# An LSTM followed by a convolution and a scan: the last pieces of the second layer laid out anew, a polynomial logarithm, one scan per 128 columns

## What is computed

```
# layer 0: LSTM, 512 strictly serial steps
a = x_t @ Wx + b + h @ Wh            # Wh: 512 x 2048
i, f, o = sigmoid(a[:3 blocks]); g = tanh(a[last block])
c = f*c + i*g ; h = o*tanh(c)
y = x + h
# layer 1: 8-tap convolution per feature (taps are the 8 rows of cond), projections, a first-order scan
conv = conv_b + sum_k y[t-7+k] * cond[k]
B_t, C_t = softplus(conv @ Wp[:, :64] + bp), tanh(conv @ Wp[:, 64:] + bp)
u = y @ Ws + bs                       # 64 states
s = decay*s + dt*B_t*u ; z = C_t*s
out = y + z @ Wo + bo
```

## Time and profile before

| | |
|---|---|
| median of three runs | 1904.51 us |
| the profiled execution | 1906.64 us, its span 1904.8 us, 1.84 us outside the span |
| TensorE matmul busy | 1812.7 us, 95% |
| VectorE busy | 1426.2 us, 75% |
| ScalarE busy | 1120.7 us, 59% |
| GpSimd busy | 337.9 us, 18% |
| mean granted TensorE clock | 0.993 of full |

### The profile page before, as it was taken

How to read it: one execution, slowest core, us unless ns; L and a number is a source line. 1 busy time by engine, 2 the same in 40 slices (tenths; PEclk the granted TensorE clock), 3 DMA queues, 4 the chain that set the end, 5 groups by cost and what they waited for, 6 DMA issues and landing times.

```text
span 1904.8 us, 124385 instructions
## 1 busy us (share of the span) xinstructions
PE 1812.7 (95%) x52738; PEld 1421.0 (75%) x52738; DVE 1426.2 (75%) x7431; ACT 1120.7 (59%) x4565; POOL 337.9 (18%) x1544
## 2 busy tenths in 40 slices
PE   6888999999999999999999999999999999999976
PEld 3666777777777777777777777777777777777865
DVE  8787667777777777777777777777777787867675
ACT  5655565565656656565565656566555566656453
POOL 1111111111111111111111111111111111111110
PEclk9999999999999999999999999999999999999997
DMA  6111111111111211111111111111111121211100
GB/s 235 55 46 39 50 49 44 47 56 41 54 54 40 63 46 51 54 46 54 46 57 46 55 48 48 55 51 54 45 54 51 41 62 44 66 38 52 44 19 20
DMA packets 112292, 100.74 MB, mean 53 GB/s; under 512 B 20225, under 2 KB 86069, under 8 KB 110710
## 3 DMA queue, kind: packets, MB, share of 16 engines
q1 hardware_dynamic: 111448, 90.70, 15.7%
q10 hardware_dynamic: 288, 2.10, 0.3%
HBM read 50.77 MB, written 41.94 MB: 49 GB/s over the span
## 4 chain that ended last, share of the span: by engine, by line
PE 72%; DVE 11%; ACT 11%; issue 3%; POOL 2%; DMA 1%; SPq 0%; POOLq 0%; DVEq 0%; ACTq 0%
PE recA L546 27%; PE recB L553 16%; PE pw L505 12%; PE pbc L630 12%; ACT act L831 5%; DVE tr L954 4%; ACT recA L757 3%; DVE pre L963 2%; POOL h L472 2%; DVE hz L989 2%; ACT tc L846 1%; PE pu L603 1%; PE pw L489 1%; PE po L650 1%; DMA wpk<-in_L_cond_Wh_dram 1%
## 5 line engine op out<-in xcount | busy, mean ns | idle before, releaser
L831 ACT ACTIVATE act<-pre 128x64 f32<-128x64 f32 (+1 forms) x1024 | 255.7, 250 | 720.0 <-DVE pre L963 712.2
L553 PE MATMUL recB<-wlo,hz 128*32 128x128 f16 x16352 | 577.8, 219 | 1.4 <-issue 1.4
L553 PE MATMUL recB<-whi,hz 128*32 128x128 f16 x16352 | 577.6, 219 | 0.7 <-issue 0.7
L546 PE MATMUL recA<-whi,hz 128*16 128x256 f16 x8176 | 515.8, 274 | 59.6 <-DVE hz L989 51.0
L546 PE MATMUL recA<-wlo,hz 128*16 128x256 f16 x8176 | 512.6, 273 | 0.1
L553 PEld LDWEIGHTS recB<-whi,hz 128*32 128x32 f16 x16352 | 438.1, 97 | 9.5
L553 PEld LDWEIGHTS recB<-wlo,hz 128*32 128x32 f16 x16352 | 438.2, 97 | 4.1 <-issue 1.9
L546 PEld LDWEIGHTS recA<-whi,hz 128*16 128x16 f16 x8176 | 199.9, 88 | 288.2 <-DVE hz L989 265.8
L954 DVE STREAM_TRANSPOSE tr<-recA 128x256 f32<-128x256 f32 x512 | 229.8, 449 | 201.0 <-PE recA L546 198.8
L630 PE MATMUL pbc<-yt,wpk 128*128 128x256 f32 (+5 forms) x1120 | 330.8, 401 | 0.0
L472 POOL TENSOR_TENSOR h<-osc,tc 128x16 f32<-128x16 f32 x1024 | 226.8, 221 | 450.2 <-ACT tc L846 450.2
(11 more groups left out here) (166 smaller groups left out, 2167.2 us busy)
## 6 DMA issues: line engine op xcount, KB each, us to landing
xw_rows<-xs SPq DMA_DIRECT2D x128, 256.0 KB, 2.3
seed<-xw_rows SPq DMA_DIRECT2D x1008, 32.0 KB, 2.0
xn<-in_x_dram SPq DMA_DIRECT2D x32, 256.0 KB
out_dram<-ot SPq DMA_DIRECT2D x32, 256.0 KB, 3.0
seed<-in_L_cond_Wh_dram ACTq DMA_DIRECT2D x2, 1024.0 KB, 7.0
wpk<-in_L_cond_Wh_dram SPq DMA_DIRECT2D x2, 1024.0 KB, 12.7
wlo<-in_L_cond_Wx_dram SPq DMA_DIRECT2D x2, 1024.0 KB, 13.9
xs<-in_L_cond_Wx_dram SPq DMA_DIRECT2D x1, 1024.0 KB, 10.1
```

Source lines behind the costliest of these rows:

```text
L546: ins = pe.matmul(rec[0][32 * j:32 * j + 2 * NB, 0:256].rearrange("p (c f) -> p c f", c=2), h[:, 2 * NB:4 * NB], w[:, k, :, :].rearrange(" ...
L553: ins = pe.matmul(rec[1][32 * j:32 * j + 32, 0:128], h[:, 2 * NB * (1 - c):2 * NB * (1 - c) + 32], w[:, k, 4 * (2 + c) + j, :], start=Fals ...
L831: act_eng.activation(act[q][:, q:G, :].rearrange("p g n -> p (g n)"), pre[q][:, q:G, :, :].rearrange("p g c b -> p (g c b)"), ACT.Tanh, sc ...
```

## The change

What it does:

1. The logarithm becomes a polynomial of degree 10 in s itself: `top` and nine `term` with fitted constants, then `sum`. `den`, `rcp`, `w`, `w2` are gone.
2. `drive` writes its product batch by batch instead of step by step. A new instruction `carry` adds decay times the last state to the first column of each batch. The scan then runs from zero over 128 columns at once; its multiplier row `dec` is zero at each batch's first column. A 256-column piece has two scans, a half piece one. `ys` reads the states back with strides.
3. The last y additions are at t = 507 (four steps), 509 (two), 510 and 511 (one each).
4. The convolutions of pieces 13 and 14 are given as 64 matmuls of 128 columns instead of 32 of 256. The last piece has 32 matmuls of 128 columns, in order of their taps: 5, 6, 7 and 10 in slots 508 to 511, and 4 in slot 512, the last tap, ahead of `y_u`.
5. The last pieces get slots of their own (the table `NEAR_END`), ScalarE's and VectorE's jobs are placed one by one against their costs, and the projections of the last groups move with `pe_load`. Worked out from the planner's code, the lists differ from slot 396 on:

| | before | after |
|---|---|---|
| conv 12, slots | 421 to 436 (2 each) | 419 to 427 (2), 428 to 441 (1) |
| conv 13 | 453 to 468 (2) | 445 to 466 (3 halves each) |
| conv 14 | 482 to 492 (3) | 471 to 490 (3 halves), 491 (5 halves) |
| `y_u` of piece 14 | 483 (all four) | 488 to 491 |
| VectorE jobs of piece 14 | 494 to 500 | 494 to 502 |
| conv 15 | 496 to 502 (5) | 495 to 501 (5) |
| VectorE jobs of piece 15 | 503 to 507 | 502 to 510 |
| most projections in one slot, 469 to 491 | 8 | 6 |
| output of steps 496 to 511 | slots 509, 510 and 513, 517 | slots 508, 513 and 513, 514 |

6. In the last slot ScalarE takes `abs` and `sig` before `u`.

Its core:

```diff
+    LOG1M = (1.0, 0.5000016093254089, 0.3332335352897644, 0.25240495800971985, ...)
+    SERIES = len(LOG1M) - 1
...
+        def y_steps(t):
+            if t >= T - 2:
+                return [t]
+            if t == T - 3:
+                return [t - 1, t]
+            return list(range(t - HS + 1, t + 1)) if (t + 1) % HS == 0 else []
...
         def conv_order(i):
             n, a, e, cols = span(i)
-            if i < NP - 1:
-                return [(c, k, a, e) for k in range(TAPS) for c in range(KC)]
-            reach = [min(e, e - HS + TAPS - 1 - k) for k in range(TAPS)]
-            return ([(c, k, a, reach[k]) for k in range(TAPS) for c in range(KC)] +
-                    [(c, k, reach[k], e) for k in range(TAPS) for c in range(KC) if reach[k] < e])
+            taps = [(c, k) for k in range(TAPS) for c in range(KC)]
+            size = TB if i < LAST - 1 else TT
+            return [(c, k, lo, lo + size) for lo in range(a, e, size) for c, k in taps]
...
-            return ["abs", "sig", "pos"], ["den"] + ["rcp"] * rcp_parts(key) + ["w", "w2", "top"] + ["term"] * SERIES + ["sum"]
+            return ["abs", "sig", "pos"], ["top"] + ["term"] * SERIES + ["sum"]
...
-            return ["u"] + on_act + ["c"] + on_dve + ["drive"] + ["scan"] * NB + ["ys"]
+            on_act = ["u"] + on_act + ["c"] if i < NP - 1 else ["abs", "sig", "u", "pos", "c"]
+            return on_act + on_dve + ["drive", "carry"] + ["scan"] * (span(i)[3] // 128) + ["ys"]
...
+        NEAR_END = {LAST - 2: ([(0, 18, 3, 2), (18, 32, 12, 1)], 20, 26, 0.65),
+                    LAST - 1: ([(0, 64, -3, 3)], 12, 18, 0.65),
+                    LAST: ([(0, 32, -9, 3), (32, 59, 2, 3), (59, 64, 11, 5)], 8, 12, 0.9),
+                    LAST + 1: ([(0, 32, -1, 5)], 2, 5, 0.8)}
...
+                conv_when[i] = [(0, 5, T - 4, 5), (5, 11, T - 3, 6), (11, 18, T - 2, 7), (18, 28, T - 1, 10),
+                                (28, jobs, T, KC)]
...
                 if name == "drive":
...
-                    dve.scalar_tensor_tensor(sp[:, 0:cols], sp[:, 0:cols], dtv[:, 0:1], us[:, 0:cols],
-                                             ALU.mult, ALU.mult).then_inc(s_drive, 1)
+                    dve.scalar_tensor_tensor(by_batch(acc[:, 0:cols]), by_step(sp[:, 0:cols]), dtv[:, 0:1],
+                                             by_step(us[:, 0:cols]), ALU.mult, ALU.mult).then_inc(s_drive, 1)
+                elif name == "carry":
+                    if i:
...
+                        first = acc[:, 0:cols:e - a]
+                        dve.scalar_tensor_tensor(first, st[:, (i - 1) % 2, ahead - 1:NB * ahead:ahead], decay[:, 0:1], first,
+                                                 ALU.mult, ALU.add).then_inc(s_drive, 1)
                 elif name == "scan":
...
-                    ins = dve.tensor_tensor_scan(st[:, i % 2, 0:e - a, z], dec[:, 0:e - a], sp[:, z:cols:NB], init,
+                    some = slice(128 * z, 128 * z + 128)
+                    ins = dve.tensor_tensor_scan(st[:, i % 2, some], dec[0 if e - a == TB else 1][:, :], acc[:, some], 0.0,
                                                  ALU.mult, ALU.add)
```

More of the change, by code:

```diff
@@ L87, in lstm_ssm_kernel @@
         sg = sb("sg", [N, COLS])
-        w2 = sb("w2", [N, COLS])
         acc = sb("acc", [N, COLS])
         ct = sb("ct", [N, COLS])
-        st = sb("st", [N, 2, TB, NB])
+        st = sb("st", [N, 2, COLS])
         ys = sb("ys", [N + 1, 2, COLS])
-        dec = sb("dec", [N, TB])
+        dec = [sb(f"dec{z}", [N, 128]) for z in range(2)]
         dtv = sb("dtv", [N, 2])
@@ L237, in lstm_ssm_kernel @@
                 dve_load[ev_when(g) + 2 + part] += 0.34
-        DVE_COST = {"den": 0.33, "rcp": 0.46, "w": 0.34, "w2": 0.34, "top": 0.34, "term": 0.44, "sum": 0.44,
-                    "drive": 0.44, "scan": 0.2, "ys": 0.35}
+        DVE_COST = {"top": 0.34, "term": 0.44, "sum": 0.44,
+                    "drive": 0.44, "carry": 0.1, "scan": 0.4, "ys": 0.35}
+        DVE_COST_HALF = {"top": 0.25, "term": 0.32, "sum": 0.32, "drive": 0.38, "carry": 0.2, "scan": 0.46, "ys": 0.3}
         ACT_AT = {"u": 0, "abs": 1, "sig": 1, "pos": 2, "c": 2}
@@ new lines, in lstm_ssm_kernel @@
+            base = TB * n + e
+            if i == NP - 1:
+                conv_when[i] = [(0, 5, T - 4, 5), (5, 11, T - 3, 6), (11, 18, T - 2, 7), (18, 28, T - 1, 10),
+                                (28, jobs, T, KC)]
+                u_when[i] = [T] * KC
+                post_at[i] = [T + 1] * len(post_order(i))
+                slot = T + 2
+                continue
+            if i in NEAR_END:
+                conv_plan, u_first, slot, room = NEAR_END[i]
+                conv_when[i] = [(lo, hi, base + first, rate) for lo, hi, first, rate in conv_plan]
+                u_when[i] = [base + u_first + k for k in range(KC)]
+                slot += base
+            else:
+                conv_when[i] = [(0, 13, base + 3, 1), (13, 21, base + 16, 2), (21, jobs, base + 20, 1)]
+                u_when[i] = [base + 27 + k for k in range(KC)]
+                slot, room = base + 31, 0.65
@@ new lines, in lstm_ssm_kernel @@
+            act_at = ACT_AT if e - a == TB else {"u": 0, "abs": 0, "sig": 0, "pos": 1, "c": 1}
+            if i == LAST - 1:
+                act_at = dict(ACT_AT, c=4)
+            post_at[i] = [slot + act_at[name] for name in post_order(i)[:len(act_at)]]
+            slot += act_at["pos"]
+            for name in post_order(i)[len(act_at):]:
+                cost = (DVE_COST if e - a == TB else DVE_COST_HALF)[name]
+                while dve_load[slot] + cost > room:
+                    slot += 1
+                dve_load[slot] += cost
+                post_at[i].append(slot)
@@ L270, in lstm_ssm_kernel @@
+            if n < NBLK - 6:
+                slot = base + 60
+            elif i not in NEAR_END:
+                slot += 3
+            elif i == LAST - 1:
+                slot = base + 43
+            elif i == LAST:
+                slot -= 1
+            for z in range(2):
+                if TT * z < e and a < TT * z + TT and (a <= TT * z):
+                    slot = min(slot + 3, T - 1)
                     while evacuates(slot):
                         slot += 1
-                    out_when[n, z] = (slot - 2, slot - 1, slot)
@@ L273, in lstm_ssm_kernel @@
[L273 to L292, removed]
+                    out_when[n, z] = (slot - 2, slot - 1, slot) if e - a == TB else (T - 4, T + 1, T + 1)
@@ L628, in conv @@
                 if last >= 0:
-                    pe.wait_ge(s_yadd, (TB * n + last) // HS + 1)
+                    pe.wait_ge(s_yadd, y_done(TB * n + last))
                 ins = pe.matmul(pbc[:, NB * (lo - a):NB * (hi - a)], wpk[:, k, c, :],
@@ L656, in beside @@
                 for i in range(NP):
+                    for lo, hi, first, rate in conv_when[i]:
+                        for j in due(t, first, rate, hi - lo):
+                            conv(i, lo + j)
                     for k in range(KC):
@@ L992, in output @@
             def output(t):
-                n = t // TB
+                n, steps = t // TB, y_steps(t)
                 if t == HS - 1:
@@ L997, in output @@
                     dve.wait_ge(s_xlow, 2 * n + 1)
[L998 to L1001, removed]
+                at = HALO + NB * (steps[0] % TB)
+                y = yt[:, n % XR, :, at:at + len(steps) * NB]
+                first = steps[0] % HS
+                dve.scalar_tensor_tensor(y, h32[:, :, first:first + len(steps), :].rearrange("p k s b -> p k (s b)"),
+                                         0.5 / SC, y, ALU.mult, ALU.add).then_inc(s_yadd, 1)
             def y_halo(n):
@@ L1024, in soft @@
                 S = lambda a: a[:, 0:cols]
-                if name == "den":
+                if name == "top":
                     dve.wait_ge(s_ssig, key + 1)
[L1027 to L1040, removed]
+                    dve.tensor_scalar(S(acc), S(sg), LOG1M[SERIES], None, ALU.mult).then_inc(s_ser, 1)
                 elif name == "term":
@@ L1122, in _ @@
             dve.memset(ys[N:N + 1, :, :], 1.0).then_inc(s_ones, 1)
-            dve.memset(dec[:, :], 1.0).then_inc(s_dec, 1)
+            for z in range(2):
+                dve.memset(dec[z][:, :], 1.0).then_inc(s_dec, 1)
+            dve.wait_ge(s_dec, 2)
+            for z in range(2):
+                dve.memset(dec[z][:, 0:128:TB >> z], 0.0).then_inc(s_dec, 1)
             for q in range(2):
```

80 lines of the change are left out of this document (29 added, 51 removed).

## The result

The changed kernel takes **1896.18 us** (median of five runs, 1895.59 to 1897.25) against 1904.87 (five runs, 1903.36 to 1908.45). The ratio is 0.9953, with a 95% interval of 0.9938 to 0.9967. It is faster, by 0.47% instead of the 0.98% forecast, and lies outside the forecast's range. The profiled execution took 1895.59 us, its span 1893.7.

The account below looks back on a forecast made before the run. The prediction took the 3.53 us recurrence loop through TensorE, VectorE, ScalarE and GpSimd as the bound. Its terms summed to -19.0 us, 0.3 given back: -18.7, from median 1904.51 to 1885.8 us, range 1881.5 to 1892.0.

Parts of the forecast that it names:

- The sign: Whole kernel: faster by over 3.8 us at 96%, within that 1%, slower 3%.
- the place of the gain: Mid-kernel closed to this change, bound by the 3.53 us recurrence; the end is where it can act.
- the forecast's five terms: Slots 482 to 492 -2.2 us, 493 to 501 -3.9, 502 to 507 -4.3, 508 to 510 -1.9, tail -6.7.
- The TensorE formula: Every step: the larger of 3.53 us and 2.07 plus 0.235 per projection, 0.43 per convolution, 0.22 per half, and other jobs.
- The tail: From the last transposition to the end: 4.8 + 4.7 + 6.0, given as 15.6 us against 22.3, -6.7.
- The rival with exposed weight loads: Slots 445 to 465 and 471 to 490: a half convolution costs like a whole, 0.43 us; +26 us, 1912; 3%.
- The 428 ns for a half convolution: Half convolutions: 2 x (107 + 107) ns by the skill's weight-load rule; the prediction held the row with 0.22 us against it.
- Up to slot 395: Slots up to 395: TensorE lists the same, VectorE's changed list hidden by its idle time; no change in time.
- to get going: Projections behind the recurrence's block in a step: about 0.2 us once, then 0.235 each.
- The clock: Rival, slots 492 to 508: clock falls, two to five half-clock steps at 0.9 us each; 1887.5 to 1890.5; 10%.
- A new queue wait: Rival: piece 14's first convolution waits for piece 13's late `c`, or strided writes cost double; 1890 to 1894; 8%.
- the polynomial alone counts: Rival, tail: narrow convolutions were hidden already, so the tail gives only 2 us; 1890; 2%.

Follow-up runs that it names:

- e8: Changed kernel with `y_u` split in two portions, one behind the convolutions, one behind the slot's first projection (or at the slot's end): 1922.53 us, ratio 1.0097.
- e1: Changed kernel with `y_u` ahead of the convolutions again in all slots but the last (512): 1887.43 us, ratio 0.9908 to the kernel before.
- e4: Kernel before with only the last convolution's part (32 matmuls of 128 columns, its y additions, `y_u` behind it in slot 512): 1899.45 us, ratio 0.9983.
- e3b: Kernel before with only polynomial, `carry` and 128-column scans, output slots pinned to those before: 1902.39 us, ratio 1.0000.
- e3: Kernel before with only polynomial, `carry` and 128-column scans, output slots left to the planner: 1915.20 us, ratio 1.0056.
- e5: Changed kernel with `y_u` of slots below 512 last in its slot, behind the projections: 1886.10 us, ratio 0.9898 to the kernel before.
- e9: Kernel before with the new VectorE instructions and the last convolution with its y additions, on the old plan: 1898.26 us, ratio 0.9973.
- e2: Kernel before with only the convolutions of a slot moved ahead of its `y_u` (slot 512 keeps the old order): 1912.34 us, ratio 1.0035.

## Why the prediction was wrong

**The sign, the place of the gain and the end were right.** Slots 482 to 510 and the tail gained 138.5 - 121.2 = 17.3 us; the forecast's five terms there sum to 19.0. The TensorE formula (2.07 plus 0.235, 0.43 and 0.22 for each job) met the new slots: three halves with four projections were forecast at 3.67 and took 3.67 or 3.68. (The tail's sum 4.8 + 4.7 + 6.0 is 15.5, not 15.6.) The rival with exposed weight loads is out by that. The 428 ns for a half convolution were the prediction's estimate, which adds load and matmul. The Trainium skill, "TensorE: Matmul & The Clock Gate", section "LDWEIGHTS (loading the stationary operand)", gives the duration of a load alone; the trace does not agree with adding it, as a half convolution takes 0.22 us here.

**The failed step is the term "Up to slot 395": "The TensorE lists are the same. ... Nothing."** The lists were the same, their order within a slot was not. The jobs of a slot were compared as sets; the hunk in TensorE's `beside` that turns them was not priced. Nor would the prediction's formula have shown it, as it charges the 0.2 "to get going" once a slot. e8 shows that it is paid at each return from narrow to wide matmuls: 0.43 against 0.23. Undone, it gives the kernel 0.9953 - 0.9908 = 0.45% or 8.6 us, of the 10.4 by which the forecast of 1885.8 was missed. By the two intervals that difference is good to about 4 us; the steps of the two traces say 7.8, which is surer. e1's 1887.43 lies 1.6 above the forecast.

**The same "Nothing" was wrong on VectorE too, by less.** The prediction took the new list for hidden because it fits. The long steps at fixed places sum to 3.6 us with the new VectorE program and to 1.9 with the old, +1.7, though the list fits. That e1 still met 1190.2 against 1190.4 in slots 60 to 394 is luck of the profiled execution before with its long steps at 91, 118 and 379; e4, with the old VectorE program and the old order, took 1187.9.

**The tail** is right by its steps: 3.42 us for the 14 half convolutions of slots 511 and 512 together, ScalarE's `abs` at 1882.02 - 1877.80 = +4.2 (forecast +4.1), VectorE at +5.0 (+4.8), `top` to `ys` 5.0 (4.7: `drive`, `carry` and `ys` were each taken 0.06 to 0.08 too cheap, the rest by less), and 6.0 from there. The changed kernel's chain, with the lines left out that repeat nine times:

```profile
1878.52 3.42 PE pbc L645 x28
...
1882.02 0.37 ACT av L777
...
1882.76 0.23 DVE acc L1043
...
1886.18 0.43 DVE acc L1065
...
1887.35 0.38 DVE ys L1090
...
1887.77 1.97 PE po L665 x4
```

**The rivals.** The clock did not fall in slots 492 to 508 (granted clock 1.00); it stood at 1.00 up to the final `ys` and was 0.52 over the output matmuls and what follows them. Before, it had fallen earlier, from 1888 us on, under the narrow convolutions. So part of the 5.06 us that the change took away was half clock: the same records took 3.70 in e3b. After:

```profile
1882.00:1887.70 5.70, 2.23 (x24) 1.50 (x22) 4.46 (x15) 2.50 (x7) 0.00 (x0) 1.00 0.17 46
1887.70:1893.70 6.00, 1.96 (x4) 1.07 (x4) 0.02 (x1) 0.60 (x1) 0.00 (x0) 0.52 0.17 44
```

A new queue wait did appear, once, for 0.6 us (slot 502), not at the place named. That the polynomial alone counts is out: the tail gave 6.4 us and not 2, and e4, without the polynomial, takes 3.3 off it.

## What to carry to other kernels

When a loop over jobs is reordered to serve one slot, price it in all slots that run the loop: compare the order of each engine's instructions, not the set. On TensorE keep jobs with narrow stationary tiles next to each other, since each return to 128 columns cost 0.2 us here wherever it stood. Where a planner derives one job's place from another's end, a shorter list moves other work; pin it before judging the shorter list (1915 against 1902 us).

## What was not expected of the hardware

Single long steps recur at fixed places, and the places follow VectorE's program. In the changed kernel slot 216 takes 3.9 us, before 3.5:

```profile
L969 DVE STREAM_TRANSPOSE tr<-recA x2: 450/450/451, 817.3 to 821.2; 128x256 f32<-128x256 f32 x2
```

```profile
L954 DVE STREAM_TRANSPOSE tr<-recA x2: 450/450/450, 816.0 to 819.6; 128x256 f32<-128x256 f32 x2
```

All kernels with the new VectorE instructions (the changed kernel and e1, e3, e3b and e5 to e9) have 3.7 to 3.9 us at the same slots (96, 103, 110, 117, 145, 202, 209, 216, 259, 287, 301, 308, 336, 358, 393), whatever was done to TensorE's order or plan. The kernel before, e2 and e4 share another set (151, 172, 193, 200, 207, 214, 228, 235, 242, 346, 374). e3b differs from the kernel before in VectorE's part alone, so it is that part that moves them. The first set sums to 3.6 us over an ordinary step, the second to 1.9. In slot 216 of the changed kernel the first low half of `h` (line 1004) starts 2.41 us into the step, where it starts at 2.06 in slot 217, though the GpSimd and VectorE results that it reads ended at the same times, 2.03 and 1.94, in both. What VectorE waits for there was not tried.

A stepped operand of a 256-column instruction cost 0.18 us on VectorE as an output (`drive`) and 0.19 as one of two inputs (`ys`), and two halves of a 64-column matmul in different columns of the array take 0.37 us together and 0.36 alone.
